# Attention outputs as three products of halves, and half of the query exponentials by ScalarE head by head, in a fused attention and mixing kernel

## What is computed

```python
qh = softmax(Wq @ layernorm(x), over the 64 rows of a head) * SCALE     # 8 heads
kh = softmax(Wk @ ctx, over the tokens)
context = einsum('bhdn,bhen->bhde', kh, Wv @ ctx)
out = Wo @ einsum('bhde,bhdn->bhen', context, qh) + bo
x = x + out / norm(out over channels) * g * sqrt(256)
# then a second layer: logits from x, 50 rounds of Sinkhorn on 4x4 matrices,
# a branch product of 512x512, and a mix of four streams
```

## Time and profile before

| | us |
|---|---|
| median of 3 runs (2566.2 to 2570.11) | 2569.74 |
| time of the profiled execution | 2568.32 |
| span in its trace | 2566.6 |
| PE busy | 2413.9 |
| DVE busy | 1726.8 |
| ACT busy | 1172.8 |
| POOL busy | 1094.4 |

### The profile page before, as it was taken

One profiled execution on the slowest core, in us unless ns is written; L12 is line 12 of the kernel. 1 busy time (PEld: TensorE's weight loads), 2 busy tenths in 40 slices (PEclk: granted clock), 3 DMA queues, 4 the chain that ended last, 5 costly groups with the idle time before them and its releaser, 6 DMA issues.

```text
span 2566.6 us, 35379 instructions
## 1 busy us (share of the span) xinstructions
PE 2413.9 (94%) x12004; PEld 1914.3 (75%) x12004; DVE 1726.8 (67%) x4114; ACT 1172.8 (46%) x2464; POOL 1094.4 (43%) x1107
## 2 busy tenths in 40 slices
PE   7999999999999999999999999999999999899774
PEld 6888878887878778787877778777778876777521
DVE  4454567676767557776776567667687756877786
ACT  4454444545354444545444454544445344453333
POOL 1635536172635427262543616245272633623410
PEclk9999999999999999999999999999999999999887
DMA  7112221313122432312213243343302233231376
GB/s 237 50 66 99 74 92 56 108 41 103 63 70 96 128 119 83 113 62 70 95 67 99 80 153 93 120 141 101 123 34 90 92 114 117 76 117 44 88 221 193
DMA packets 200145, 255.72 MB, mean 100 GB/s; under 512 B 43550, under 2 KB 109854, under 8 KB 199966
## 3 DMA queue, kind: packets, MB, share of 16 engines
q1 hardware_dynamic: 199966, 253.47, 31.3%
HBM read 177.53 MB, written 75.89 MB: 99 GB/s over the span
## 4 chain that ended last, share of the span: by engine, by line
PE 57%; DVE 20%; POOL 11%; issue 8%; ACT 3%; SPq 1%; DMA 1%; DVEq 0%; POOLq 0%; ACTq 0%
PE kc_bank L642 15%; PE big L701 7%; PE tb L743 4%; PE tb L757 3%; PE tb L628 3%; PE big L616 3%; PE big L618 3%; PE big L617 3%; POOL x_tr L1535 3%; DVE stats L889 3%; PE big L675 3%; PE big L677 2%; PE big L676 2%; PE tb L686 2%; POOL q_sb L1515 2%
## 5 line engine op out<-in xcount | busy, mean ns | idle before, releaser
L1254 ACT COPY turned<-tb 128x512 f32<-128x512 f32 x512 | 298.7, 587 | 755.3 <-PE tb L686 487.9
L701 PE MATMUL big<-merged,turned 128*128 128x256 f32 x2048 | 495.0, 385 | 36.3 <-ACT turned L1254 24.5
L642 PE MATMUL kc_bank<-ctxt,turned 128*128 128x256 f32 x2048 | 479.5, 380 | 3.0 <-DMA ctxt<-in_ctx_t 3.0
L701 PEld LDWEIGHTS big<-merged,turned 128*128 128x128 f32 x2048 | 385.8, 191 | 110.7 <-ACT turned L1254 19.4
L642 PEld LDWEIGHTS kc_bank<-ctxt,turned 128*128 128x128 f32 x2048 | 374.6, 191 | 54.6 <-issue 8.9
L1490 POOL TENSOR_TENSOR in_l<-x_sb,in_h 128x512 fp32r<-128x512 f32 x128 | 167.8, 1340 | 574.9 <-ACT in_h L1294 574.8
L1515 POOL TENSOR_TENSOR q_sb<-q_sb,qsum 128x1024 f32<-128x1024 f32 x128 | 243.8, 1904 | 274.4 <-DVE qsum L971 274.4
L980 DVE SCALAR_TENSOR_TENSOR on<-big,nrm,g_rows 128x256 f32<-128x256 f32 x256 | 111.9, 479 | 220.7 <-POOL nrm L1528 220.4
L616 PE MATMUL big<-in_h,wk_h 128*128 128x512 f32 x512 | 237.7, 464 | 15.4 <-DVE in_l L821 10.0
L675 PE MATMUL big<-wq_h,in_h 128*128 128x512 f32 x512 | 236.4, 462 | 10.9 <-DVE q_sb L959 10.4
L757 PE MATMUL tb<-mix_ld,mix_w 121*96 121x512 f32 (+2 forms) x324 | 187.9, 677 | 57.7 <-POOL mix_w L1497 28.0
(11 more groups left out here) (149 smaller groups left out, 4308.5 us busy)
## 6 DMA issues: line engine op xcount, KB each, us to landing
mix_ld<-streams SPq DMA_DIRECT2D x157, 240.0 KB
ctxt<-in_ctx_t SPq DMA_DIRECT2D x64, 512.0 KB, 4.0
x_sb<-in_x SPq DMA_DIRECT2D x64, 512.0 KB, 6.1
x_tr<-in_x_t SPq DMA_DIRECT2D x64, 512.0 KB, 6.6
streams<-x_sb SPq DMA_DIRECT2D x64, 512.0 KB, 3.1
stage<-in_ctx SPq DMA_DIRECT2D x60, 512.0 KB, 4.1
out<-mix_out SPq DMA_DIRECT2D x157, 192.0 KB, 2.2
streams<-y_sb SPq DMA_DIRECT2D x32, 256.0 KB, 2.0
```

Source lines behind the costliest of these rows:

```text
L642: t = nc.tensor.matmul(kc_bank[:, 0:C], turned[n % 3][:, j * P:(j + 1) * P], ctxt[:, nt, :], start=nt == 0, stop=nt == NT - 1)
L701: t = nc.tensor.matmul(big[2 + p % 2][:, half], turned[n % 3][:, dt * P:(dt + 1) * P], merged[:, dt, :], start=dt == 0, stop=dt == DT - 1)
L1254: nc.scalar.copy(turned[k % 3][:], tb[n % 2][:]).then_inc(s_tba, 1)
```

## The change

Three things change.

1. The attention output of a tile is twelve products of float32r halves instead of four in float32. ACT's `turn` casts the transposed tile to `turned_h`, DVE's new `query_low` subtracts it from the bank to make `q_low`, and `merged` becomes `merged_h` and `merged_l`, for which DVE does three operations in the place of one. `SPLIT` is 16, so this holds for all batches. A `tb` bank of a query tile comes free with `query_low`, not with `turn`.
2. For the pairs 1, 3, 5 and 7 of each batch (`SCALAR_PAIRS`), the subtraction, the exponential over a pair, POOL's halves and DVE's sum go: DVE writes the negated maxima `qneg`, and ACT's new `query_soft` computes the exponential of each head from the bank, with the maximum as bias and the sum of the head as accumulator: 8 instructions of 128x64 for a tile, at steps 2p and 2p + 1.
3. PE transposes tile i - 4 ahead of the attention output of tile i - 5, not behind it.

Some buffers share their place now: `q_low` lies in `k_exp`, `pre_t` in `q_sb`; the first exponentials of the keys of the next batch wait for the last attention output. The core of the diff:

```diff
+    SPLIT = NB
+    SCALAR_PAIRS = [b < SPLIT and k % 2 == 1 for b in range(NB) for k in range(PAIRS)]
@@ attention_out
+                if b < SPLIT:
+                    w.wait_ge(s_low, LOW_READS["fg", n])
+                    w.wait_ge(s_mrg, 2 * (b + 1) * DT)
+                    for dt in range(DT):
+                        high = turned_h[:, n % 3, dt * P:(dt + 1) * P]
+                        nc.tensor.matmul(bank, high, merged_h[:, dt, :], start=dt == 0, stop=False)
+                        nc.tensor.matmul(bank, high, merged_l[:, dt, :], start=False, stop=False)
+                        t = nc.tensor.matmul(bank, low_of(n)[:, dt * P:(dt + 1) * P], merged_h[:, dt, :], start=False,
+                                             stop=dt == DT - 1)
@@ tensor_program, step i
+                    if 4 <= i < NT + 4 and b < SPLIT:
+                        query_transpose(b, i - 4)
                     if 5 <= i < NT + 5:
                         attention_out(b, i - 5)
...
@@ chain_bank, k == 2
-                    nc.vector.tensor_tensor(merged[:, dt, :], bank[:, 0:C], bo_heads[:], ALU.add).then_inc(s_tbv, 1)
+                        nc.vector.tensor_tensor(merged_h[:, dt, :], bank[:, 0:C], bo_heads[:], ALU.add).then_inc(s_mrg, 1)
+                        w.wait_ge(s_mrg, 2 * n + 1)
+                        nc.vector.tensor_tensor(chain_t, bank[:, 0:C], f32(merged_h[:, dt, :]), ALU.subtract).then_inc(s_tbv, 1)
+                        w.wait_ge(s_tbv, VECTOR_READS["chain", b, dt, 2])
+                        nc.vector.tensor_tensor(merged_l[:, dt, :], chain_t, bo_heads[:], ALU.add).then_inc(s_mrg, 1)
@@ query_subtract
+                if SCALAR_PAIRS[p]:
+                    return
@@ new, VectorE, at step i + 5 behind query_subtract
+            def query_low(b, i):
+                n = b * FG + DT * NQ + i
+                if i == 0:
+                    w.wait_ge(s_tb, TB["fg", n - 1] + 1)
+                w.wait_ge(s_use, n - 2)
+                w.wait_ge(s_tba, SCALAR_READS["fg", n])
+                nc.vector.tensor_tensor(low_of(n), tb[TB["fg", n] % 2][:], f32(turned_h[:, n % 3, :]), ALU.subtract).then_inc(s_low, 1)
@@ query_sum
+                if SCALAR_PAIRS[n]:
+                    w.wait_ge(s_qacc, 2 * scalar_pairs(n + 1))
+                else:
+                    w.wait_ge(s_half, vector_pairs(n + 1))
+                    nc.vector.tensor_reduce(qsum[:, p % 2, 0, :], qhalf, AX_X, ALU.add).then_inc(s_qsum, 1)
@@ new, ScalarE, at the head of step i, ahead of query_exp
+            def query_soft(b, i):
+                p, j = i // 2, i % 2
+                n = b * PAIRS + p
+                w.wait_ge(s_qmax, b * NT + i + 1)
...
+                for h in range(HEADS):
+                    cols = slice(h * DIM_HEAD, (h + 1) * DIM_HEAD)
+                    k = j * HEADS + h
+                    t = nc.scalar.activation(q_sb[n % QB][:, j, cols], big[j][:, cols], ACT.Exp, bias=qneg[:, j, h:h + 1],
+                                             accum_out=qsum[:, p % 2, 0, k:k + 1])
+                t.then_inc(s_qacc, 1)
```

More of the change, by code:

```diff
@@ L342, in xattn_ffn @@
         ctxt = sb("ctxt", [P, NT, C])
-        k_exp = sb("k_exp", [P, N])
-        turned = [sb(f"turned{i}", [P, BANK]) for i in range(3)]
+        with nc.sbuf_tensor("k_exp", [P, N], F32) as k_exp:
+            pass
+        q_low = sb("q_low", [P, 4, BANK], F32R)
+        with nc.sbuf_tensor("turned", [P, 3, BANK], F32) as turned_all:
+            pass
+        turned_h = sb("turned_h", [P, 3, BANK], F32R)
+        turned = [turned_all[:, i, :] for i in range(3)]
         on = sb("on", [P, 2, C])
@@ L697, in attention_out @@
                         w.wait_ge(s_scl, (b * PAIRS + p - 1) * 2)
-                w.wait_ge(s_tba, SCALAR_READS["fg", n])
-                w.wait_ge(s_tbv, VECTOR_READS["chain", b, DT - 1, 2])
-                for dt in range(DT):
-                    t = nc.tensor.matmul(big[2 + p % 2][:, half], turned[n % 3][:, dt * P:(dt + 1) * P], merged[:, dt, :],
-                                         start=dt == 0, stop=dt == DT - 1)
+                bank = big[2 + p % 2][:, half]
+                if b < SPLIT:
[7 more added lines that the diff above has]
+                                             stop=dt == DT - 1)
+                else:
+                    w.wait_ge(s_tba, SCALAR_READS["fg", n])
+                    w.wait_ge(s_tbv, VECTOR_READS["chain", b, DT - 1, 2])
+                    for dt in range(DT):
+                        t = nc.tensor.matmul(bank, turned[n % 3][:, dt * P:(dt + 1) * P], merged[:, dt, :],
+                                             start=dt == 0, stop=dt == DT - 1)
                 t.then_inc(s_use, 1)
@@ L1220, in vector_program @@
                         query_subtract(b, i)
+                    if b < SPLIT and 5 <= i < NT + 5:
+                        query_low(b, i - 5)
                     if i == 1:
@@ L1569, in pool_program @@
                         query_normalise(b, (i - 3) // 2)
-                    if i >= 2 and i % 2 == 0 and i < NT + 2:
+                    if i >= 2 and i % 2 == 0 and i < NT + 2 and not SCALAR_PAIRS[b * PAIRS + (i - 2) // 2]:
                         query_half(b, (i - 2) // 2)
```

82 lines of the change are left out of this document (64 added, 18 removed).

## The result

| | before | with the change |
|---|---|---|
| median, us (range) | 2568.18 (2566.2 to 2570.11) | 2643.02 (2642.77 to 2644.19) |
| ratio, with its 95% interval | | 1.0292 (1.0275 to 1.031) |
| profiled execution: time, us | 2568.32 | 2642.89 |
| its span, us | 2566.6 | 2641.2 |
| its span less PE's busy time, us | 152.7 | 257.7 |

The forecast was 2547 us in a range of 2495 to 2620. The change is slower, and above the range.

What follows compares the result with a forecast made beforehand. PE was taken to bound the kernel, with DVE close behind in nine batches and setting the pace in two. 2568.3 - 74 (products) - 12 (transposes) + 37 (openings) + 28 (DVE) = 2547 us, range 2495 to 2620.

Steps and rivals of the forecast that it cites:

- What bounds the kernel: Query stages: PE bounds the kernel, with DVE close behind in nine batches and setting the pace in two.
- the three kinds of batches: Five bound by PE alone (0, 1, 5, 9, 13), nine with DVE close behind, two paced by DVE (14, 15).
- DVE keeps up: Faster rival: DVE's idle and port waits shrink with POOL's work, so the 28 us are not paid; 2519 us, chance 0.18.
- The products: Outputs on PE: twelve products at 0.12 us make 1.44 us a tile for 1.73, -74 us over 256 tiles.
- at nothing: Effects given no cost: PE's float32r/float32 moves, smaller POOL work, the next batch's first key exponential, ACT's extra work.
- Transposes ahead: On PE ahead of the outputs: hides the 24.5 us wait for `turned`, half counted because of `query_low`, -12 us.
- The opening: Start of each query stage: the exponential behind the heads delays the first output, 2.3 us in 16 batches, +37 us.
- DVE, taken at +28: Query stages: DVE too full to follow PE's saving, 18 us in nine batches and 10 in batches 14 and 15.
- Slower: the sum waits behind the heads in every second pair: Rival: on ACT even pairs' exponentials stand behind heads, so DVE's sum waits; 2591 us, chance 0.30.
- The 2645 at its far end: Slower rival with heads at 3.8 us a tile: the opening adds 27 us and the pairs as much again.
- DVE has no slack: Condition of the slower rival: the late sum decides once DVE has no slack, 4 us in each of eleven batches.
- C: Theory from the follow-up runs, not the prediction: ACT's queue costs time in batches where it also copies mixes.

Runs made afterwards that it cites:

- e2: The change with ACT's exponential over a pair put ahead of the next tile's heads, all else the same: 2582.63 us, ratio 1.0071.
- e4: The kernel before with only the transposes moved ahead of the outputs, no heads, float32 outputs: 2556.06 us, ratio 0.9962.
- e7: The change with the transposes of a tile behind the output of the tile before, as before the change: 2717.61 us, ratio 1.0591.
- e1: The change without its scalar pairs (no heads), outputs still products of halves: 2649.64 us, ratio 1.0326.
- g1: e2 with `q_low` computed for 128 of 512 columns and read four times in the third product: 2563.03 us, ratio 0.9985.
- 5 rounds: e2 with 5 Sinkhorn rounds in the place of 50: 2479.97 us; with 5 rounds the change took 2515.49 and the kernel before 2482.31.
- e5: The kernel before with transposes ahead and heads behind the exponential of a pair, outputs in float32: 2551.22 us, ratio 0.9936.
- e6: e2 with float32 outputs in the last two batches, heads and transposes ahead in all: 2562.96 us, ratio 0.9986.
- e8: e2 with ACT computing the exponentials of four heads in one instruction, two a tile for eight: 2562.11 us, ratio 0.9985.
- f1: e5 with heads left out in batches 0, 1, 6, 10 and 11: 2531.85 us, ratio 0.9863.

## Why the prediction was wrong

**What bounds the kernel** was read rightly, and the three kinds of batches too. What failed is how DVE would limit PE: as an engine that gets full. By the prediction DVE would be over 95% busy in batch 6. It was busy 32.55 of 40 us, 81%. Batches 5, 9 and 13, taken as bound by PE alone and thus as gaining, lost 3.7, 3.6 and 6.8 us.

Part of the busy time that the forecast added to was no work. The product of two tiles of SBUF (the memory beside PSUM) in a Sinkhorn step takes 0.29 us in the 85 cases of this size in which no POOL operation runs when it starts. Where one runs on for over 0.2 us, it takes up to 1.78 (the median of 54 is 1.51), and ends about 0.15 us behind that operation. In the kernel before:

```profile
959.95 1.90 POOL L1515 TENSOR_TENSOR q_sb<-q_sb,qsum 128x1024 f32<-128x1024 f32 x1 [1.97 <-DVE qsum L971]
...
960.33 1.67 DVE L1061 TENSOR_TENSOR skw<-skq,ska 128x128 f32<-128x128 f32 x1
```

Of the 35.6 us of the earlier trace rows in batch 6, 7.0 are such lengthening of five of these products, so that DVE had some 28.6 us of work there. The rival "DVE keeps up" named this, and the forecast gave it 0.18.

**The products, taken at -74 us.** The timeline in batch 6 with the change, beside the earlier trace rows:

```profile
1007.57 0.66 PE L732 MATMUL tb<-ident,q_sb 128*128 128x128 f32 x4 [0.44 <-DVE q_low L1046]
1007.98 0.36 PE L750 MATMUL big<-merged_h,turned_h 128*128 128x256 f32 x1
1008.18 0.28 PE L751 MATMUL big<-merged_l,turned_h 128*128 128x256 f32 x1
1008.30 0.28 PE L752 MATMUL big<-merged_h,q_low 128*128 128x256 f32 x1
...
1009.37 0.28 PE L752 MATMUL big<-merged_h,q_low 128*128 128x256 f32 x1
1009.49 0.60 PE L777 MATMUL kc_bank<-ident,x_tr 128*128 128x128 f32 x4
```

A product of 256 columns takes 0.12 us (1008.18 to 1008.30), as taken. "TensorE: Matmul & The Clock Gate" of the Trainium skill, section Back-to-back issue gap, gave an estimate of 0.109; the row was the better guide. But the first one takes 0.20, so twelve make 1.51 and not 1.44. Summed over the trace from start to start, with idle left out, the outputs take 405 us (454 before), everything into `tb` 20 more, the first products of the logits 5 less: 33 us gained (48 - 20 + 5) and not 74. Of the 41 missing, the first product is 256 x 0.08 = 20. That is a term that I had "at nothing", PE's move between float32r and float32. It isn't made as often as before, either: PE goes from float32 to float32r 460 times in the trace before and 573 times with the change, since an output in float32 stood next to other float32 products and one in halves does not. The rest stays open. The four transposes here take 0.41 us (1007.57 to 1007.98), but they had stood; in 154 of 256 tiles their median is 0.36, as before. In sum they take 16 us more, and half of that is gone in e2, which has the same products in the same places, so it is not all a cost of the change of kind. Short waits that the overlap of two records hides would count as busy; whether the rest is such waits is not shown.

**Transposes ahead, taken at -12.** By itself -10 (e4), so the size was about right for a kernel with float32 outputs. I had seen that `q_low` stands behind the wait, and only halved the gain for it. With the products the move is worth 77 us (e7), 47 of it in PE's wait for `q_low`.

**The opening, taken at +2.3 us each, 37 in all.** The steps are in the trace as described. Batch 1, all engines:

```profile
225.25 0.68 DVE L1019 TENSOR_REDUCE qneg<-big 128x8 f32<-128x512 f32 x1
225.97 0.32 ACT L1369 ACTIVATE q_sb<-big,qneg 128x64 f32<-128x64 f32 x1 [6.62 <-DVE qneg L1019]
226.18 0.19 ACT L1369 ACTIVATION_READ_ACCUMULATOR q_sb<-big,qneg 128x1 f32 x1
226.27 0.31 ACT L1369 ACTIVATE q_sb<-big,qneg 128x64 f32<-128x64 f32 x1
...
228.30 1.10 ACT L1354 ACTIVATE q_sb<-q_sb 128x1024 f32<-128x1024 f32 x1
228.50 0.50 PE L721 MATMUL big<-wq_h,in_h 128*128 128x512 f32 x1 [1.40 <-ACT q_sb L1369]
...
230.78 0.69 DVE L1054 TENSOR_REDUCE qsum<-x_pre 128x16 f32<-128x512 f32 x1 [1.98 <-POOL x_pre L1621]
...
236.80 0.39 PE L750 MATMUL big<-merged_h,turned_h 128*128 128x256 f32 x1 [0.52 <-DVE q_low L1046]
```

Heads are 0.30 us apart (225.97 to 226.27), mostly 0.29, where I took 0.26: 2.3 us a tile and not 2.1. "ScalarE: Activation LUTs" of the Trainium skill, section What ACT_TABLE_LOAD costs, gave an estimate of 0.33; the measurement lies between. The first output comes 24.8 us after the start of the stage (236.80 less 212.0), 21.2 before: 3.6 us later, for 2.7 forecast. But the order on ACT is not what makes it: e2, in the other order, opens at 23.8, and e1, without heads, at 24.3, where e4 has 21.6. So `q_low` and the three operations for `merged` cost 2.7 us by themselves (e1 less e4), and the late exponential adds 1.0 (change less e2). The number came near by a chain of which the later links alone were enough. In batches 0 and 1 the later opening is paid by a shorter run of outputs, 54.4 us for 58.0 before in batch 1, so that the batch is as long as before and nothing remains of the 2 us that I expected. I had the logits wait for `q_sb` of ACT in the opening only in part: 1.40 us here and 35.8 us in all, which I had put at nothing.

**DVE, taken at +28.** This is the step that failed in mechanism. The forecast asked how much work DVE would have per tile and found 36.9 us in 36.8. What counts is which of DVE's instructions PE waits for, and what is queued ahead of that one. `q_low` is a third hand-over between PE's transposes and PE's outputs (PE, ACT, DVE, PE instead of PE, ACT, PE), on an engine whose queue also holds the sum, the maxima and the Sinkhorn steps. Each of these can be late for a reason of its own, and the outputs are then late with it. PE stands 119.5 us for `q_low` (100.8 and 18.7), while DVE is idle for 32% of the span; as a share of time it looked free. That the length of this way counts, and not DVE's load alone, is what e7 shows; how the two share the wait is not shown (g1).

**The rival that held.** "Slower: the sum waits behind the heads in every second pair" had 0.30, and its sign appeared: DVE idle ahead of `qsum` for 85.8 us. e2 takes out exactly this and 57 us go; with its 5 rounds the order still costs 35.5. Its price, 2591 us with heads at 2.1 us a tile, put 44 us on the forecast where 96 were due: I charged 4 us in eleven batches and let PE keep the gain of the products. The 2645 at its far end rested on heads at 3.8 us, which were 2.3, so that the nearness of 2643 is a coincidence. What I missed is the link from the late sum to `q_low` behind it (batch 7 above). The point "DVE has no slack" was not needed either.

**The balance.** In PE's time, the forecast had 74 us less work and 53 more waiting (37 + 28 - 12). Measured were 30 less and 105 more. So 44 of the 96 us between forecast and result are work that PE was to lose and kept, nearly all of it in the products' term, and 52 are waits. By the runs, in this order of adding (another order would share them otherwise):

| step | us |
|---|---|
| transposes ahead (e4) | -10 |
| heads behind the exponential (e5 less e4) | -7 |
| the three products (e2 less e5) | +35 |
| the exponential behind the heads (change less e2) | +57 |
| in all | +75 |

**What stays open.** e6, e8 and g1 each take 22 us from e2, and whether these are the same 22 us was not tried. C was formed on lengths of batches and one timeline, and it missed its range in e5, e6 and e8. That f1 came out as expected (2533 and 2531.85 us) shows that the lengths of batches add up, and not why the heads cost in those three; batches 14 and 15 have as many mix copies, and heads pay there. ACT's mix copies were never moved or taken away by themselves. The three operations for `merged` and `q_low` were not tried apart. The places that buffers share with the change (`q_low` in `k_exp`, `pre_t` in `q_sb`) were the same in every version and have no run of their own. And the float32r pieces were not tried with heads only where they pay, beyond batches 0 and 1.

## What to carry to other kernels

When a stage goes to another engine, ask not only whether that engine has time, but what is queued ahead of the new instruction and how late that can be: here DVE stood idle in a third of its time while PE waited for it. A split of one instruction into eight is put behind the short work that others wait for, not ahead of it; two lines in another order were worth 57 us. And take a change apart by the kind of batch it meets: the moved transposes and the heads, behind the exponential, made 0.6% when used throughout (e5) and 1.4% when the heads were chosen by batch (f1). Last, look whether an instruction's busy time is the same each time: what is stretched by a wait inside it isn't work, and a sum that treats it as work finds an engine full that is not.

## What the runs showed of the hardware

- A float32r product of 256 columns is 0.12 us from start to start, and 0.20 where it comes first after float32 transposes. The trace of before shows the same for 512 columns. The first of the logits after the transposes starts at 970.10, the next two as follows, so 0.32 us for the first and 0.23 for the second:

```profile
970.42 0.39 PE L676 MATMUL big<-wq_l,in_h 128*128 128x512 f32 x1
970.65 0.40 PE L677 MATMUL big<-wq_h,in_l 128*128 128x512 f32 x1
```

- An exponential of 64 columns with a bias and an accumulator's read is 0.29 to 0.30 us from start to start, of which the read spaces the next by 0.09.
- A DVE product of two SBUF tiles of 128x128 takes 0.29 us, and 1.51 in the median where a POOL operation is running when it starts and goes on for over 0.2 us; it ends about 0.15 us after that operation. The profile counts all of it as busy. In the trace of before this one line, with its tiles of 128x64, is lengthened by some 67 us in sum.
- The granted clock was 1.00 in the stretch of batch 14 before and 0.96 with the change, where PE stood more in between (33.10 of 40 us busy); over the whole trace it went from 0.982 to 0.972. What this adds to the time was not measured.
